# Mixing of the first mixture's outputs moved from a stage of its own into the second layer's projection stage

## The reference

```python
    x = _layernorm(x + _L0_ffn_ref(...))     # 64 experts, 8 per token, at most 128 tokens per expert
    x = _layernorm(x + _L1_attn_ref(...))
# end of _L0_ffn_ref
        slot_out = yb[dest] * topk_w.reshape(-1)[:, None].astype(yb.dtype)
        out = jnp.zeros((T, h), yb.dtype).at[slot_token].add(slot_out)
# start of _L1_attn_ref
        proj = x @ W_in.T                    # 512 -> 2 x 1024
        xs, z = jnp.split(proj, 2, axis=-1)
        ...                                  # causal convolution of 4 taps over xs
        u = silu(conv)
        x_dbl = u @ W_x.T                    # dt_r 128, Bm 16, Cm 16
        dt = jax.nn.softplus(dt_r @ W_dt.T + b_dt)
```

## Time and profile before

| | |
|---|---|
| median of 3 runs | 5336.33 us (5331.58 to 5353.86) |
| the profiled execution | 5341.18 us, its span 5339.5 us |
| PE, DVE, ACT, POOL busy in the span | 76%, 54%, 30%, 26% |
| TensorE's granted clock, mean | 0.88 |
| gather stage, first DMA to the next stage's | 2795.1 to 3011.6 us |
| projection stage, the same | 3011.6 to 3404.5 us |

### The profile page before, as it was taken

The page is one execution under the profiler, slowest core; times in us unless marked ns, Lnnn a source line. Parts: engine busy times, 40 slices in busy tenths (PEclk is TensorE's granted clock), DMA queues, the critical chain, the costliest instruction groups (busy, mean ns, idle before and its releaser), DMA issues. The chain is left out here.

```text
span 5339.5 us, 61460 instructions
## 1 busy us (share of the span) xinstructions
PE 4043.5 (76%) x19166; PEld 3086.1 (58%) x19166; DVE 2866.6 (54%) x5082; ACT 1596.6 (30%) x3253; POOL 1412.9 (26%) x1223
## 2 busy tenths in 40 slices
PE   7985999979998878537980288577777758845993
PEld 6884777767777436433440267455555546634772
DVE  6663344444444329651225644599999945542335
ACT  4432222232221110011210255555555522212332
POOL 0002100000000007561007300499999900002002
PEclk9997999989999989758995599898989989977996
DMA  4235522232222541228965353644546021124324
GB/s 134 89 115 191 168 83 58 80 95 83 75 63 68 197 172 45 91 84 279 317 228 175 97 115 121 164 84 76 110 90 99 20 92 54 45 81 115 115 95 119
DMA packets 474924, 611.59 MB, mean 115 GB/s; under 512 B 116038, under 2 KB 352391, under 8 KB 467601
## 3 DMA queue, kind: packets, MB, share of 16 engines
q1 hardware_dynamic: 417168, 490.72, 31.7%
q0 software_dynamic: 44544, 106.42, 6.6%
q10 hardware_dynamic: 13056, 12.59, 0.7%
HBM read 440.76 MB, written 210.73 MB: 122 GB/s over the span
## 5 line engine op out<-in xcount | busy, mean ns | idle before, releaser
L2086 PE MATMUL d_py<-d_h,d_ident 128*128 128x256 f32 x2048 | 538.0, 421 | 182.2 <-POOL d_h L1926 160.9
L1934 POOL TENSOR_TENSOR d_dBu<-d_B,d_dtu 128x1024 f32<-128x1024 f32 x256 | 597.1, 2365 | 34.1 <-DMA d_dtu<-dtu 34.1
L2086 PEld LDWEIGHTS d_py<-d_h,d_ident 128*128 128x128 f32 x2048 | 426.8, 212 | 293.4 <-POOL d_h L1926 189.8
L715 PE MATMUL a_pB<-a_uhi,a_whi 128*128 128x512 f32 x1152 | 488.5, 424 | 40.4 <-DVE a_ulo L598 40.4
L715 PE MATMUL a_pB<-a_uhi,a_wlo 128*128 128x512 f32 x1152 | 462.1, 401 | 0.0
L715 PE MATMUL a_pB<-a_ulo,a_whi 128*128 128x512 f32 x1152 | 459.2, 399 | 0.0
L1972 ACT ACTIVATE d_ph<-d_dt,d_A 128x255 f32<-128x255 f32 x1024 | 425.7, 460 | 0.2
L2032 DVE TENSOR_TENSOR_SCAN d_ph<-d_ph,d_dBu 128x1024 f32<-128x1024 f32 x160 | 365.7, 2286 | 17.7 <-POOL d_dBu L1934 12.0
L1004 POOL TENSOR_TENSOR b_kv<-b_c 128x128 f32 (+11 forms) x256 | 100.2, 429 | 864.4 <-DMA b_c<-ctx_turned 861.0
L715 PEld LDWEIGHTS a_pB<-a_uhi,a_whi 128*128 128x128 f32 x1152 | 223.4, 194 | 82.6 <-issue 30.0
L682 DVE SCALAR_TENSOR_TENSOR a_W<-a_pG,a_cB,a_M 128x256 f32<-128x256 f32 (+1 forms) x384 | 142.7, 413 | 227.9 <-PE a_pG L736 127.2
(11 more groups left out here) (458 smaller groups left out, 9522.7 us busy)
## 6 DMA issues: line engine op xcount, KB each, us to landing
c_gu<-w_gu SPq DMA_DIRECT2D x64, 768.0 KB, 4.7
a_wraw<-w_bc SPq DMA_DIRECT2D x24, 1536.0 KB
a_alall<-alpha SPq DMA_DIRECT2D x24, 1024.0 KB, 5.9
slots<-a_zeros POOLq DMA_DIRECT2D x64, 256.0 KB, 3.3
c_wd<-w_down SPq DMA_DIRECT2D x64, 256.0 KB, 5.1
c_xb<-slots SPq DMA_DIRECT2D x64, 256.0 KB, 7.6
slots_y<-c_y POOLq DMA_DIRECT2D x64, 256.0 KB
f_w1r<-w SPq DMA_DIRECT2D x64, 256.0 KB, 2.7
```

Source lines behind the costliest of these rows:

```text
L715: ins = nc.tensor.matmul(out, a[:, k, cols], b[:, k, ts], start=(k == 0 and n == 0), stop=(k == F - 1 and n == 2))
L1934: pool.tensor_tensor(dBu[c % RB][:, :, :], B_sb[i][:, q * G:(q + 1) * G, :], dtu_sb[i][:, f, :].unsqueeze(1).to_broadcast([P, G, L]), ALU. ...
L2086: ins = nc.tensor.matmul(py[f % 2][:, 0:L], ident_sb[:, :], h_sb[c % RH][:, n, :], start=False, stop=(q == Q - 1 and n == G - 1))
```

## The change

`gather_mix_norm` is no longer called for the first mixture, and the x3 feature copy is gone. `ssm1_project` becomes `mix_project`. Its batch `b` projects tokens and, among the groups of channels, mixes and normalises the tokens of batch `b + 1`: `SHARE[f]` says which of its 16 mixings (two tiles, eight experts) DVE does after the convolution of group `f`; moments, root, scaling, transposes and the split into `x_hi` and `x_lo` stand at fixed groups too. There is one gather buffer per expert slot `k`, and POOL issues the next gather into it once it was read. The tokens of batch 0 are mixed between the chunks of the weight split, which has four buffers now instead of six. `pr` and `pb` share one bank and one semaphore; dt and dtu are written over r and v; the B and C stores move to SP; `bc1` is laid out by batch, so that a batch's B is one contiguous row; and the spreading of the first batch's B and C moves from POOL after batch 0 to ACT's queue in the last batch.

```diff
-def ssm1_project(nc, first_bc, x_feat, ...):
-    WBUF = 6
+def mix_project(nc, first_bc, y_slots, x_in, places, weights, ident, ...):
+    WBUF = 4
+    MOMENTS_AT, SCALE_AT, ROOT_AT, TURN_AT, PARTS_AT = (2, 5), (3, 6), (3, 6), (5, 7), (6, 7)
+    SHARE = ((0, 1, 2), (3, 4, 5), (6, 7), (8, 9, 10), (11, 12, 13), (14, 15), (), ())
...
+        g = [m.sb(f"g{k}", [P, D]) for k in range(K_)]
-        pr, pb = m.ps("pr"), m.ps("pb")
+        prb, po = m.ps("prb"), m.ps("po")
+        pr, pb = prb[:, 0:L], prb[0:2 * N1, L:2 * L]
...
         def _(pool):
+            pool.wait_ge(s_set, 4 + K_)
+            with pool.Fori(0, NB // 2) as r:
+                for i in range(2):
+                    b = 2 * r + i
+                    pool.wait_ge(s_in[i], r * 48 + 48)
+                    for c in range(2):
+                        for k in range(K_):
+                            pool.wait_ge(s_mix, (b * 2 + c) * K_ + k + 1)
+                            alone(pool, tick_pool)
+                            pool.indirect_dma_start(g[k][:, :], None, y_slots, bass.IndirectOffsetOnAxis(ap=pl[i][:, c, k:k + 1], axis=0),
+                                                    bounds_check=SLOTS - 1, oob_is_err=False).then_inc(s_g[k], 16)
...
+            def root(t, c):
+                act.wait_ge(s_var, t + 1)
+                nc.scalar.activation(sd[:, c:c + 1], mv[:, c, 1:2], ACT.Sqrt, bias=eps_sb[:, :], scale=1.0).then_inc(s_sd, 1)
...
+                if not more(b):
+                    act.wait_ge(s_out, 16)
+                    for dst, at in ((first_bc.B, 0), (first_bc.C, N1 * L)):
+                        act.dma_start(dst[:, :, :].rearrange("p n t -> p (n t)"), bc_feat[0, at:at + N1 * L].partition_broadcast(P)).then_inc(first_bc.loaded, 16)
                 biased(b)
...
+            def mixed(b, n, i):
+                c, k = n // K_, n % K_
+                x = xm[i][:, c, :]
+                dve.wait_ge(s_mix, b * 2 * K_ + K_ + n)
+                dve.wait_ge(s_g[k], (b * 2 + c) * 16 + 16)
+                nc.vector.scalar_tensor_tensor(x, g[k][:, :], wk[i][:, c, k:k + 1], x, ALU.mult, ALU.add).then_inc(s_mix, 1)
...
+            for c in range(2):
+                for n in range(c * K_, c * K_ + K_):
+                    chunk(n)
+                    mixed(0, n, 0)
+                moments(0, c, 0)
+                scaled(0, c, 0)
+                parts(0, c, 0)
...
-                    if f == SPLIT_AT + 1 and more(b):
-                        split(b + 2, 1 - i)
                     a, xp = acc[f % 2], xpad[f % 2]
...
+                    if more(b):
+                        if f == 0:
+                            dve.wait_ge(s_in[1 - i], (r + i) * 48 + 48)
+                        for c in range(2):
+                            if f == SCALE_AT[c]:
+                                scaled(b + 1, c, 1 - i)
+                        for n in SHARE[f]:
+                            mixed(b + 1, n, 1 - i)
+                        for c in range(2):
+                            if f == MOMENTS_AT[c]:
+                                moments(b + 1, c, 1 - i)
+                            if f == PARTS_AT[c]:
+                                parts(b + 1, c, 1 - i)
-                dve.wait_ge(s_pr, b + 1)
-                nc.vector.tensor_copy(dr_sb[:, :], pr[:, 0:L]).then_inc(s_dr, 1)
                 dve.wait_ge(s_pb, b + 1)
+                nc.vector.tensor_copy(dr_sb[:, :], pr).then_inc(s_dr, 1)
...
-    gather_mix_norm(nc, "c3", K_, slots_y, SLOTS, x2_tok, places0, weights0, a["ident"], x3_tok, x3_feat)
-    bc1 = scratch("bc1", 2 * N1, T)
+    bc1 = scratch("bc1", NB, 2 * N1 * L)
```

More of the change, by code:

```diff
@@ new lines, in _ @@
+            normed(0, 0)
+            project(0, 0, 0, None)
+            with sp.Fori(0, NB // 2 - 2) as r:
+                for i in range(2):
+                    b = 2 * r + 1 + i
+                    project(b, r + i, 1 - i, lambda b=b: step_sizes(b - 1))
+            for b in (LAST - 2, LAST - 1):
+                project(b, b // 2, b % 2, lambda b=b: step_sizes(b - 1), ahead=b + 2 < NB)
+            project(LAST, NB // 2 - 1, 1, lambda: step_sizes(LAST - 1), ahead=False)
+            step_sizes(LAST)
@@ L1627, in _ @@
+            for s in (s_out, s_out_u, s_out_z, s_dts, s_out_dtu):
+                sp.wait_ge(s, NB * 16)
+            for i in range(2):
+                sp.wait_ge(s_xo[i], NB // 2 * 16)
+        @block.gpsimd
+        def _(pool):
+            pool.wait_ge(s_set, 4 + K_)
+            with pool.Fori(0, NB // 2) as r:
                 for i in range(2):
                     b = 2 * r + i
-                    load(b + 2, i)
-                    project(b + 1, None, 1 - i, lambda b=b: step_sizes(b))
@@ L1652, in _ @@
[L1652 to L1658, removed]
+            act.wait_ge(s_set, 4)
+            def root(t, c):
+                act.wait_ge(s_var, t + 1)
+                nc.scalar.activation(sd[:, c:c + 1], mv[:, c, 1:2], ACT.Sqrt, bias=eps_sb[:, :], scale=1.0).then_inc(s_sd, 1)
@@ L1676, in project @@
                         nc.scalar.copy(xpad[f % 2][:, 3:3 + L], px[f % 2][:, 0:L]).then_inc(s_xpad, 1)
-                    if f == SPLIT_AT and more(b):
-                        act.wait_ge(s_pz, b * F1)
-                        split((r + i) * 16 + 16, 1 - i)
+                    if more(b):
+                        if f == ROOT_AT[0]:
+                            root(b * 2 + 2, 0)
+                        if f == ROOT_AT[1]:
+                            root(b * 2 + 3, 1)
+                        if f == PARTS_AT[0]:
+                            act.wait_ge(s_pz, b * F1)
+                            parts(b * 2 + 2, 0, 1 - i)
                     if f >= 1:
@@ L1705, in _ @@
             nc.vector.memset(one_sb[:, :], 1.0).then_inc(s_set, 1)
-            dve.wait_ge(s_set, 3)
-            dve.wait_ge(s_const, 16 * CONSTS)
-            def split(turn, i):
-                dve.wait_ge(s_xh, turn)
-                nc.vector.tensor_tensor(x_lo[i][:, :, :], xT[i][:, :, :], x_hi[i][:, :, :].bitcast(F32), ALU.subtract).then_inc(s_xl, 1)
-            split(1, 0)
-            for n, (k, cols) in enumerate(CHUNKS):
+            nc.vector.memset(eps_sb[:, :], LN_EPS).then_inc(s_set, 1)
@@ new lines, in _ @@
+            dve.sem_inc(s_mix, K_)
+            for k in range(K_):
+                nc.vector.memset(g[k][:, :], 0.0).then_inc(s_set, 1)
+            dve.wait_ge(s_set, 4 + K_)
+            def mixed(b, n, i):
[4 more added lines that the diff above has]
+                nc.vector.scalar_tensor_tensor(x, g[k][:, :], wk[i][:, c, k:k + 1], x, ALU.mult, ALU.add).then_inc(s_mix, 1)
@@ L2760, in decoder @@
     x2_tok = scratch("x2_tok", T, D)
-    x3_tok, x3_feat = both("x3")
+    x3_tok = scratch("x3_tok", T, D)
     with ExitStack() as across:
```

127 lines of the change are left out of this document (95 added, 32 removed).

## The result

The changed kernel takes 5242.2 us (median of 4, 5240.85 to 5250.79), the kernel before 5338.1 (median of 4 beside it, 5331.58 to 5353.86). The ratio is 0.9819 with a 95% interval of 0.9803 to 0.9835: faster by 1.8%. The profiled execution has a span of 5240.8 us against 5339.5, so 98.7 us have to be found.

What follows compares the result with a forecast made beforehand. DVE was taken to bound each batch's convolution phase, then idle in the tail. Terms -216.5 + 15.6 + 105.1 + 8.6 + 1.9 + 0.6 - 9.2 = -93.9 gave a forecast of 5245 us, range 5222 to 5284.

Steps and rivals of the forecast that it cites:

- A batch: Full projection batches 1 to 6: 60.0 us instead of 42.46, +17.5 each, 105.1 for the six.
- The second rival: DVE is not kept busy in its blocks, waiting 2 us a batch: 5266 us; chance 0.13.
- The fourth rival: Gathers land late beside the 1 MB stores and the change turns slower, up to 5474 us; chance 0.02.
- The tail: From a batch's last convolution to the next batch: 21.9 us grows by 1.9, with ends 0.6 and 5.
- the dr copy's 0.6: In the tail, the dr copy waits for pb on the shared semaphore, so pd starts 0.6 us later.
- The clock: In the tail, pr starts at PE's lower clock after a pause of some 8 us: +0.65 us.
- The rival of 1.2 GHz all stage: PE stays at the lower clock throughout the merged stage: 5325 us, no change that can be told; chance 0.04.
- The start: From the stage's first DMA to PE's first matmul: 43 us instead of 27.4, +15.6, ends +11 and +20.
- B and C: Their spread for the scan's first batch, moved to the last batch's end, is hidden at 24 us.
- the price from the alpha spread: B and C's spread priced by alpha's contiguous rows, 5.9 us for half the size: 4 x 5.9 = 24 us.
- The rival of the old rows: At the scan's start, B and C come some 20 us late, as the old spread's 49.7 us suggests: 5265; chance 0.10.
- The stall of 9.2: ACT's 9.24 us wait for the z store in batch 2 goes when the spread leaves batch 1: -9.2.

Runs made afterwards that it cites:

- e4: The changed kernel with eight of a batch's sixteen mixings moved from between the convolutions into the tail of the batch before; 5206.8 us.
- e1: The changed kernel with SP issuing five of the six constants after the last weight chunk instead of between the fourth and fifth; 5237.6 us.
- e3: The changed kernel with pr and pb in two banks and a semaphore behind pr, so DVE copies dr while PE computes pb; 5237.5 us.
- e6: The changed kernel with B and C in DRAM in the old row layout for the stores and all spreads; 5276.8 us.
- e2: The changed kernel with ACT's two roots behind the silus of their group instead of ahead of them; 5255.9 us.
- e9: The kernel of e2 with 30 unread matmuls in PE's pause ahead of the second tile's transposes, in each of batches 0 to 6; 5242.2 us.
- e11: The kernel of e10 with six buffers for raw weights instead of four; 5162.5 us.
- e7: The kernel before the change with only B and C stored in the new layout, contiguous for each batch; 5328.1 us.
- e10: The kernel of e8 with fourteen mixings in the tail instead of twelve; 5163.2 us.
- e8: The changed kernel with twelve mixings and the first tile's moments in the tail, dr copied before pb, and the constants split; 5178.0 us.

## Why the prediction was right

The median came out at 5242.2 against 5245, and the steps hold with one exception.

- **A batch.** Six full batches took 59.5 us in the mean (357.18 / 6) where 60.0 was forecast: the phase 36.3 (forecast 36.2), the tail 23.2 (23.8). That DVE bounds the phase is shown by e4: with eight mixings fewer it is 5.5 us shorter (30.3 in the mean against 35.8, the late batch left out), of 6.3 by the full price. The second rival, waits of DVE in its blocks, stayed small but for one batch: that from 3134.68 took 62.8, because ACT copied the px of group 6 at 3166.60, 3.1 us later in its batch than in batches 2 and 3. It recurs at the same batch, with 1 to 2 us, in e1, e3 and e6, and not in e2 and e9, where the root stands elsewhere. What holds ACT there stays open: PE's rows end that px at 3162.77, so PE was not late, as e2's expectation had it. The fourth rival, late gathers, did not come: behind the first gather of the start (1.97 us) DVE waits for none.
- **The tail** grew by 1.3 us in the mean (23.2 against 21.9 in the earlier trace rows), not 1.9. Of its three parts the dr copy's 0.6 is right (0.7 by e3). The last silu came 0.3 us late in the mean, by a late pz, where 0.6 was taken. The clock cost 0.35, not 0.65: the sixteen matmuls of pr took 4.53, 3.82, 3.72, 3.72, 4.61 and 4.02 us in batches 1 to 6. Some batches pay and some don't. The pause that the term rested on, some 8 us ahead of pr, was not there: PE paused 2.0 to 5.2 us, ahead of the last pz. The Trainium skill (TensorE: Matmul & The Clock Gate, HAM oscillation) has a kernel that lets TensorE wait between bursts pay at every restart. The trace agrees behind the pause of 10 to 11 us at the first root, where PE restarts at 0.50 in all six batches, and not ahead of pr, where two of six paid nothing; e2 shows that what matters is what runs at the restart. The rival of 1.2 GHz all stage did not come: the clock of the full batches is 0.86.
- **The start failed.** "The second tile has its gathers in time and costs eight pairs", 43 us, took weights for granted. SP's order, constants between the fourth and fifth chunk, and a ring of four instead of six made it 50.8. Of these 7.8 us, e1 gives back 4.0 and e11 nearly all: 43.5. The prediction costed what DVE does and not what SP must issue first. That the sum then comes out is in part luck: the eight memsets took 4.27 us, not 6.6, and in e11 the first gathered rows were there 6.3 us behind the end of their issue (2805.29 to 2811.55), not 2.8.
- **B and C.** They were hidden, as forecast; the price from the alpha spread was too high, for C landed at 13.4, not 24. The rival of the old rows was mis-sized and had the wrong mechanism: e6 shows 34.6 us, not 20, through the stores queued behind, not through the scan's wait for B and C. The stall of 9.2 is confirmed by e7, as 10.0 in batch 2 (52.43 to 42.47).
- **Outside the stage** nothing was forecast. The 7.8 us found there are within what the stretches scatter by.

In the stage the start's 7.8 us too few and the 4.8 too many of the batches leave 3.0 (-93.9 forecast, -90.9 measured). The 7.8 us outside turned that the other way. That 5245 is within 3 us of the median is therefore luck; the price of a batch, which is what the change turns on, is not.

## What to carry over

When a stage is laid beside another, look at when in a period an engine is free, and not only at how much of it: DVE was busy 163 of 365 us and still had no room in the phase, while 14 us of every tail stayed empty until the work was ordered into it (e4, 2.5% below the kernel before instead of 1.8%; e10, 3.4%). Where work moves to a new stage, write down the issue order of its DMA queue too. And before a wait is taken from PE, see where its next pause will end: a pause that ends just ahead of matmuls on the path costs more than a longer one elsewhere.

## What the runs showed of the hardware

- After PE's pause of 4.05 us the sixteen matmuls of pr took 6.73 us instead of 3.72, and thirty matmuls that nobody reads, put in the pause, gave the time back: 13.7 us over seven batches (e2, e9).
- Two broadcasts of 2 MB each, one behind the other, landed 7.7 and 13.4 us after their issue from one contiguous row each, and 29.4 and 58.1 from sixteen rows of 1 KB, 8 KB apart. Meanwhile SP took 14.07 and 12.57 us to issue two stores that take 4.31 and 0.37 in the changed kernel (e6).
- Issuing one constant of 4 KB (128 x 8 numbers, spread as single ones) took SP 4.04 us in the changed kernel, between the weights; behind them it took 3.40 in e1 and 1.19 in e8. Why is not settled.
